# Self attention in a fused decoder layer: eight of the 32 row maxima of a head are taken from a ScalarE copy and a VectorE scan, where they were one VectorE reduction

## The reference: what is computed

```
attn = jnp.einsum('bhqd,bhkd->bhqk', q, k) * SCALE
diff = pos[None, :] - pos[:, None]
diff = jnp.where(diff > 0, 0.0, diff)
attn = attn + (diff[None, :, :] * slopes[:, None, None] * MAX_BIAS)[None]
w = jax.nn.softmax(attn, axis=-1)
out = jnp.einsum('bhqk,bhkd->bhqd', w, v)
```

## Time and profile before

| | |
|---|---|
| median of 3 runs | 1970.86 us (1969.94 to 1981.66) |
| the profiled execution's own time | 1990.41 us |
| its span, first to last instruction | 1988.6 us |
| share of the span busy: TensorE, VectorE, ScalarE, GpSimd | 90%, 70%, 59%, 18% |
| mean granted TensorE clock | 0.930 |
| rounds of self attention | from about 217 us to 925 us |

### The profile page before, as it was taken

How to read it: one execution, slowest core, us unless ns; L and a number is a source line. 1 busy time by engine, 2 the same in 40 slices (tenths; PEclk the granted TensorE clock), 3 DMA queues, 4 the chain that set the end, 5 groups by cost and what they waited for, 6 DMA issues and landing times.

```text
span 1988.6 us, 30263 instructions
## 1 busy us (share of the span) xinstructions
PE 1782.0 (90%) x10422; PEld 922.6 (46%) x10422; DVE 1388.6 (70%) x2786; ACT 1176.5 (59%) x2401; POOL 356.0 (18%) x576
## 2 busy tenths in 40 slices
PE   6774899999999999998699999999999885999993
PEld 3332333333333333333454444444444265999993
DVE  7452899999999999951599999999999044110113
ACT  1111477777777777775317877777787651333332
POOL 7101122234222222211000000000000002333331
PEclk9886799999999999997859999999999886999997
DMA  7132000010000000000212010101002123777773
GB/s 266 69 117 96 2 27 27 30 36 33 32 27 26 27 27 30 23 2 21 83 45 86 26 39 22 40 25 36 30 30 78 43 91 127 203 200 198 197 200 101
DMA packets 72608, 140.14 MB, mean 70 GB/s; under 512 B 14140, under 2 KB 47309, under 8 KB 70237
## 3 DMA queue, kind: packets, MB, share of 16 engines
q1 hardware_dynamic: 64746, 127.84, 19.3%
q0 software_dynamic: 7712, 10.37, 3.2%
HBM read 109.07 MB, written 28.45 MB: 69 GB/s over the span
## 4 chain that ended last, share of the span: by engine, by line
PE 71%; DVE 13%; ACT 6%; issue 4%; DMA 3%; SPq 2%; POOL 0%; POOLq 0%; ACTq 0%; DVEq 0%
PE banks L990 21%; PE banks L977 21%; PE banks L939 8%; PE banks L1174 7%; PE banks L1184 7%; PE banks L881 4%; ACT XT L1250 4%; DVE skip L1437 2%; DVE wset L1437 2%; DVE CM L1433 2%; ACT late L1250 2%; DVE CM L1428 1%; SPq L578 1%; PE banks L950 1%; DMA kxD<-parts 1%
## 5 line engine op out<-in xcount | busy, mean ns | idle before, releaser
L1250 ACT ACTIVATE XT<-banks 128x512 f32<-128x512 f32 x1240 | 658.7, 600 | 247.4 <-PE banks L977 191.7
L939 PE MATMUL banks<-oper 52*128 52x512 f32 (+1 forms) x2048 | 717.0, 443 | 41.2 <-DMA oper<-qD 14.0
L977 PE MATMUL banks<-oper 54*128 54x512 f32 x1856 | 692.1, 458 | 33.8 <-POOL oper L752 10.5
L977 PEld LDWEIGHTS banks<-oper 54*128 54x128 f32 x1856 | 309.6, 189 | 537.7 <-ACT XT L1250 312.6
L1428 DVE TENSOR_REDUCE CM<-banks 128x1 f32<-128x402 f32 x1024 | 512.6, 566 | 33.5 <-PE banks L939 22.1
L939 PEld LDWEIGHTS banks<-oper 52*128 52x128 f32 x2048 | 352.5, 192 | 150.8 <-DVE CM L1437 55.6
L1250 ACT ACTIVATE late<-banks 128x512 f32<-128x512 f32 x616 | 327.9, 600 | 93.5 <-PE banks L977 78.9
L990 PE MATMUL banks<-XT,VS 128*32 128x512 f32 x2480 | 340.2, 621 | 1.3 <-ACT XT L1250 0.7
L1329 ACT ACTIVATE HID<-banks,b1E 128x128 f32<-128x128 f32 x312 | 85.4, 382 | 182.7 <-DMA b1E<-in_b1T_dram 164.2
L1607 DVE TENSOR_TENSOR YB<-banks,b2E 128x256 f32<-128x256 f32 x39 | 16.6, 425 | 252.1 <-PE banks L1184 252.1
L990 PE MATMUL banks<-late,VS 128*32 128x512 f32 x1232 | 169.3, 622 | 0.3
(11 more groups left out here) (204 smaller groups left out, 1395.8 us busy)
## 6 DMA issues: line engine op xcount, KB each, us to landing
W<-in_w1T_dram SPq DMA_DIRECT2D x39, 1024.0 KB
oper<-kD SPq DMA_DIRECT2D x32, 256.0 KB
W2R<-in_w2T_dram SPq DMA_DIRECT2D x8, 1024.0 KB, 7.6
oper<-kxD SPq DMA_DIRECT2D x32, 208.0 KB
b2E<-in_b_dram SPq DMA_DIRECT2D x39, 128.0 KB
qD<-parts SPq DMA_DIRECT2D x8, 512.0 KB, 2.7
kD<-parts SPq DMA_DIRECT2D x8, 512.0 KB, 2.7
oper<-kD SPq DMA_DIRECT2D x32, 128.0 KB
```

The lines of the kernel that those rows point to most:

```text
L939: mm = pe.matmul(slot[:, n * QB:n * QB + ch], QO[64 * g:64 * g + M_ROWS, c2, col:col + P], KO[64 * g:64 * g + M_ROWS, c2, k0:k0 + ch], sta ...
L977: pe.matmul(bank, KO[64 * g:64 * g + S_ROWS, c, b * P:(b + 1) * P], QO[64 * g:64 * g + S_ROWS, c, q0:q0 + QB], start=True, stop=True).then ...
L1250: act.activation(PT[(c * plan.nu + u) % PRING], S[(c * plan.nu + u) % SBANKS], ACT.Exp).then_inc(A.exps, 1)
```

## The change: what it does

Of the two items of a round, at most one is "folded": the eight plain items of a head, one in every even round. In rounds 0, 2, 4 and 6 it is item 1, in rounds 8, 10, 12 and 14 item 0. Items ahead of the first round (`h` below 0) are not folded. For a folded item ScalarE copies the slot's first bank (512 keys) to a buffer FO in SBUF, between exponentials of the round: behind the first when the folded item is item 0, behind the third when it is item 1 (`FOLD_AT`). VectorE waits for the copy, and then runs one tensor_tensor_scan over 512 columns, whose state is the maximum of the state, the slot's second bank and the copy; it waits for its own scan, copies the last column of the result to CM and frees the slot.

```diff
+FOLD_AT = (0, 2)
...
+    def folded(self, item, h):
+
+        return self.causal and item[0] == "max" and item[2] == 1 and item[1] < self.nm // 4 and h >= 0
...
+        FO = sb("FO", [P, 2, QB])
...
+        s_scan = sem("folded_half_scanned")
...
+                self.fold = sem(f"{name}_half_slot_copied")
...
                         act.activation(PT[(c * plan.nu + u) % PRING], S[(c * plan.nu + u) % SBANKS],
                                        ACT.Exp).then_inc(A.exps, 1)
                         if u == 3 and not first:
                             save(h - 1)
+                        b = u // 4
+                        for i, item in enumerate(plan.ring_items(b, h)):
+                            if u % 4 == FOLD_AT[min(i, 1)] and plan.folded(item, h):
+                                n = plan.folds_before(h, b)
+                                act.wait_ge(A.filled, pos + i + 1)
+                                if n >= 2:
+                                    act.wait_ge(A.freed, places[n - 2] + 1)
+                                act.activation(FO[:, n % 2, :], R[(pos + i) % plan.slots][:, 0:QB], ACT.Copy).then_inc(A.fold, 1)
+                        if u % 4 == 3:
+                            pos += len(plan.ring_items(b, h))
...
+                        elif plan.folded(item, h):
+                            n = places.index(pos)
+                            dve.wait_ge(A.fold, n + 1)
+                            dve.tensor_tensor_scan(FO[:, n % 2, :], slot[:, QB:2 * QB], FO[:, n % 2, :], -3.0e38,
+                                                   ALU.max, ALU.max).then_inc(s_scan, 1)
+                            dve.wait_ge(s_scan, n + 1)
+                            dve.tensor_copy(CM[:, a, b:b + 1], FO[:, n % 2, QB - 1:QB]).then_inc(A.freed, 1)
                         elif not biased:
                             dve.tensor_reduce(CM[:, a, b:b + 1], slot, AX.X, ALU.max).then_inc(A.freed, 1)
```

More of the change, by code:

```diff
@@ L151, in ring_items, with folds_before, fold_places @@
         return items
+    def folded(self, item, h):
+        return self.causal and item[0] == "max" and item[2] == 1 and item[1] < self.nm // 4 and h >= 0
+    def folds_before(self, h, b):
+        seen = sum(self.folded(i, g) for g in range(h) for i in self.head_items(g))
+        return seen + sum(self.folded(i, h) for tile in range(b) for i in self.ring_items(tile, h))
+    def fold_places(self):
+        places, pos = [], len(self.prologue)
+        for h in range(H):
+            for i in self.head_items(h):
+                if self.folded(i, h):
+                    places.append(pos)
+                pos += 1
+        return places
     def head_items(self, h):
@@ L1233, in attention @@
             def attention(A, plan):
+                places = plan.fold_places()
                 def save(h):
@@ L1242, in step @@
                     first = isinstance(h, int) and h == 0
+                    pos = plan.ring_before(h)
                     for u in range(plan.nu):
```

## The result

The changed kernel takes 2180.66 us (median of 4 runs, 2164.9 to 2184.3). Over the kernel before on the same chip that is a ratio of 1.103, with a 95% interval of 1.096 to 1.110: some 203 us slower by that ratio, and 210 us above the 1970.86 that the forecast started from, where 150 had been forecast. The forecast's point was 2121 us, so the measured median lies 60 us above it: outside the 2090 to 2150 us given as its own range, and 4 us inside the end of the whole range of 2050 to 2185. The profiled execution has a span of 2175.6 us against 1988.6. Some executions of a kernel run longer at a lower granted clock; the ratios leave them out, but the profiles of experiments 2 (2020.8 us) and 5 (2021.6 us) are of such executions.

What follows compares the result with a forecast made beforehand. VectorE's queue was taken as the bound, TensorE close behind. Folded items cost 85 + 77 us, less 12 given back: 150 us onto 1970.9, 2121 us. Whole range 2050 to 2185 us, the forecast's own 2090 to 2150.

Steps and rivals of the forecast that it cites:

- The bound: Steady self attention: VectorE's own queue bounds, TensorE close behind; ScalarE waits for VectorE's bias once a round.
- the sum: Self attention, 118 folded items: 85 us (item 0) plus 77 (item 1) less 12 given back, 150 us slower.
- The standstill: VectorE's scan waits for ScalarE's copy in folded rounds: 1.24 us with item 0, 1.07 us with item 1.
- The scan: VectorE, folded items: two steps a column, 1.22 us; with its chain 1.36 us for 1.14, 0.22 us more an item.
- The fast scan: Rival on VectorE: scan at one column a step, 0.54 us less an item, 63 us less in all; chance 0.15.
- The copy on ScalarE at nothing: ScalarE, folded rounds: 118 copies, 70 us of busy time, costed at nothing beyond the standstill.
- lost cover: ScalarE, folded rounds: if the copy's delay of exponentials were no longer covered, 0.5 us a folded round on top.
- What comes back: The usual round's 0.13 us wait for S0 goes in folded rounds: about 0.1 x 118 = 12 us regained.
- The clock: Rival: TensorE's clock falls from idle gaps in folded rounds, 114 us more, 2235 us; chance 0.10.
- the clock leaves 1.00 in the heads with maxima: Sign that the forecast is wrong; it expected granted clock 1.00 from 230 us to the end of head 13.
- My argument from the last rounds of the kernel before: Against a clock fall: gapped rounds without maxima held 1.00 for 42 us with 12 matmuls; rounds with maxima have 16.
- Not slower, the copy hidden: Rival: copy ready when VectorE comes, before 0.20 us (item 0) or 1.34 (item 1); 47 us less, 1924 us; chance 0.03.

Runs made afterwards that it cites:

- experiment 2: Changed kernel without ScalarE's copy and the wait for it, the scan's second input a constant SBUF table; ratio 1.005 to the kernel before.
- experiment 5: Changed kernel with the copy moved up and a one-step-a-column instruction replacing scan and one-column copy; ratio 1.000 to the kernel before.
- experiment 4: Changed kernel with ScalarE's copy moved ahead of the first exponential (item 0) or behind the first (item 1); ratio 1.042 to the kernel before.
- experiment 1: Changed kernel with scan and one-column copy replaced by the plain reduction, still waiting for ScalarE's copy; ratio 1.087 to the kernel before.
- experiment 6: Changed kernel, its copy left in place, with a one-step-a-column instruction for the scan and its chain; ratio 1.045 to the kernel before.
- experiment 9: Kernel before plus ScalarE copies of a constant SBUF table at the change's places, with no wait; ratio 0.999 to the kernel before.
- experiment 3: Kernel before plus ScalarE copies of the score bank the next exponential reads, at the change's places; ratio 1.011 to the kernel before.
- experiment 7: Changed kernel with the matmul of S3 issued four times more in folded rounds, filling TensorE's gaps; ratio 1.087 to the kernel before.

## Why the prediction was right, and where its size was off

**The bound** was read rightly, with one reservation. Before the change the first exponential starts 0.03 us behind the bias in every round but round 1 (medians of heads 1 to 13). But in three of the four rounds with item 0 folded (8, 10 and 14) ScalarE is also busy with the fourth exponential of the round before until that moment, and that one waits for TensorE. I hadn't seen this second hold; the sum is the same with it, and experiment 4 ran into it. Experiment 1 shows that a wait tied into that loop costs its length.

**The standstill** was forecast as 1.24 us (item 0) and 1.07 (item 1), counted from where the reduction would have started. Rounds grew by 1.50 and 1.24, where the sum had 1.46 and 1.29 less 0.1. The copies end where the sum had them, 1.42 and 2.40 us behind the start of the bias for 1.41 and 2.38. The difference lies in the hand-off from ScalarE to VectorE, 0.11 to 0.12 us (598.23 to 598.35) where I took 0.03 from the step in the other direction; counted as in the sum, the standstill of item 0 is 1.53 - 0.20 = 1.33 us. Four rounds of each kind make 4 x 1.46 + 4 x 1.29 = 11.0 us, less 0.8 that comes back 10.2; a head with the clock up shows 10.9.

**The scan** at two steps a column: 1224 ns for my 1.22 us, and 1.1 us a head by itself (experiment 2) for 8 x 0.22 less what comes back. The section "Datapath and trigger behaviour" of the Trainium skill's "DVE: opcode table, instruction layouts, handler registers and perf-mode slots", which gives half throughput, agrees with this row. The fast scan, at 2058 us, is out; experiment 6, with a one-step instruction in the same place, shows that it would not have turned the sign.

**The copy on ScalarE at nothing** holds (experiment 9). The bound that I gave for lost cover, 0.5 us a round, turned up in experiment 3: round 7 grew by 0.50.

**What comes back**, 12 us: plain rounds went from 2.61 to 2.56, and the heads fit.

**The clock** is the term that was mis-sized. I had it as a rival with a chance of 0.10 and none of it in the sum, and "the clock leaves 1.00 in the heads with maxima" stood among my own signs that the forecast is wrong. It did leave it, in nine of heads 1 to 13 and in head 14. So the wait, the scan and the path were right, and the statement on the clock was wrong; that the time still fell into the range, by 4 us, is owed to a range that allowed a short fall of the clock, and is in part luck. Lengths that go with the low clock took 37.6 of the 198.0 us. My argument from the last rounds of the kernel before, which held 1.00 for 42 us with gaps, did not carry over. Experiment 7 shows that with the gaps partly filled the clock stays up for most of heads 1 to 13 (27.5 us lost there became 4.1). The rival's price was too high: it had 4 rounds in each of 15 heads at 1.9 us, 114 us, and the profile has 27.5 us in heads 1 to 13, where a plain round at 0.50 loses 1.5 us (4.10 for 2.56) and a folded one next to nothing. The 7.7 us of head 14 are less certain: in experiment 2 the clock fell there without any standstill. The section "A second HAM failure mode: psum-queue depth-cycling" of the Trainium skill's "TensorE: Matmul & The Clock Gate" was the better guide here in kind, with the clock at 0.95 and 0.98 in the windows above; the size that I had given that rival came from my own rows and was too large.

**Sum:** 150 forecast; in the profile 160 for heads with the clock up, and 38 that go with the low clock. The hand-off is behind the first difference, 0.7 us a head. The measured 203 us come from other executions than the profiled one, and how much the clock takes in each of them was not measured. "Not slower, the copy hidden" would have needed copies that end by 0.20 and 1.34 us; they end at 1.42 and 2.40. Moving them up did not help enough (experiment 4), and even the cheapest form there (experiment 5) breaks even.

## What to carry to other kernels

Before work is moved to an engine with idle time, look at what ends that idle time: ScalarE was only 79% busy here, but it waited for VectorE in nearly every round, and the work that it took over came back to VectorE as a wait. Cost the new instruction from its dependences, not from its column count; a scan of half the columns took as long as the reduction of all. And a wait in a loop that two engines share idled the third one too, so look at what TensorE's clock may do in those gaps, and say in the forecast what it would cost.

## What was not expected of the hardware

- The clock of TensorE fell and rose several times in heads that were all alike: window means of 0.95 and 0.98 in the changed kernel, 0.99 with the gaps filled (330 to 1050 us). Four of thirteen like heads showed no loss, the longest 7.6 us. What decides it within a head stays open. Longer gaps are not the whole of it: experiment 1 has shorter rounds than the changed kernel and a fall in every head.
- In the last rounds, which have no maxima, the clock fell early in some profiles whatever had been changed before. From round 10 or 11 of head 14 on it stood at 0.50 for 75 to 99 us in experiments 1, 2, 4, 5 and 6; in the changed kernel it was 34 us, and in the kernel before 27 us, near the end of head 15. Head 15, to its last bias, then takes 59.6 to 62.8 us for 44.5. Experiments 2 and 5 have no gap of TensorE over 0.6 us there, as the kernel before. What sets it off stays open, and the ratios may carry some of it, up to 18 us in head 15, which the lengths of single heads don't. A window of experiment 5:

```profile
885.00:960.00 75.00, 69.58 (x224) 18.54 (x220) 5.96 (x20) 39.37 (x74) 5.43 (x19) 0.50 0.00 1
```

- At the start, where the clock is low, the same padding had the opposite sign: head 0 took 13 us longer. TensorE was busy 58.5 of the 60 us from 225 to 285 us, and the mean clock was still 0.62.

```profile
225.00:285.00 60.00, 58.54 (x238) 24.19 (x236) 35.30 (x68) 31.56 (x60) 3.97 (x14) 0.62 0.01 2
```

- ScalarE's copy of 512 columns took 595 to 606 ns from PSUM and 632 ns from SBUF.
